# Pool issues its own loads, W1 goes first, W2 passes through y, and the last three chunks run as two halves of 256 rows

## The reference

```
h = sigmoid(einsum('bts,st->bs', x, W1) + b1)      # x: 1024 x 24 x 1024, W1: 1024 x 24
y = h @ W2.T + b2                                  # W2: 1024 x 1024, y: 1024 x 1024, all f32
```

## Time and profile before

| | us |
|---|---|
| median of 3 runs (lowest, highest) | 336.53 (336.32, 337.71) |
| the profiled execution's own time | 337.88 |
| its span, first to last instruction | 336.1 |
| PE busy | 273.2 (81%) |
| DVE busy | 259.1 (77%) |
| POOL busy | 165.5 (49%) |
| ACT busy | 44.5 (13%) |
| HBM read / written | 105.5 MB / 4.2 MB |

### The profile page before, as it was taken

How to read it: one execution, slowest core, us unless ns; L and a number is a source line. 1 busy time by engine, 2 the same in 40 slices (tenths; PEclk the granted TensorE clock), 3 DMA queues, 4 the chain that set the end, 5 groups by cost and what they waited for, 6 DMA issues and landing times.

```text
span 336.1 us, 4849 instructions
## 1 busy us (share of the span) xinstructions
PE 273.2 (81%) x1825; PEld 238.0 (71%) x1825; DVE 259.1 (77%) x386; ACT 44.5 (13%) x76; POOL 165.5 (49%) x63
## 2 busy tenths in 40 slices
PE   2672975696977989999993899998889979299896
PEld 2572965596966877889782788876778868188674
DVE  0652997987998979799993489899788997168836
ACT  1210220211260000012300000040101140000010
POOL 0050007679059684800899980049755059972000
PEclk9978797977999999999997699999999998789979
DMA  8999959999999999999957999999999992698006
GB/s 260 398 398 393 387 183 393 386 387 387 386 386 387 387 387 387 387 384 373 373 205 244 374 375 384 383 385 374 373 373 372 356 341 81 207 345 262 1 0 250
DMA packets 67383, 109.99 MB, mean 327 GB/s; under 512 B 3224, under 2 KB 40096, under 8 KB 67360
## 3 DMA queue, kind: packets, MB, share of 16 engines
q1 hardware_dynamic: 65584, 106.96, 89.3%
q10 hardware_dynamic: 1776, 2.72, 2.2%
HBM read 105.48 MB, written 4.19 MB: 326 GB/s over the span
## 4 chain that ended last, share of the span: by engine, by line
PE 36%; DMA 35%; POOL 14%; issue 10%; ACT 2%; SPq 1%; DVE 1%; POOLq 0%; DVEq 0%; ACTq 0%
DMA ring<-in_r_x 35%; PE xbank L207 17%; PE pbank L267 15%; POOL y L463 6%; POOL nsum L446 3%; PE xbank L301 3%; POOL h_lo L456 2%; POOL nsum L451 1%; POOL nat L448 1%; PE pbank L301 1%; ACT h L392 1%; SPq L171 1%; DVE acc L323 1%; ACT h_hi L421 0%; PE pbank L225 0%
## 5 line engine op out<-in xcount | busy, mean ns | idle before, releaser
L323 DVE SCALAR_TENSOR_TENSOR acc<-xbank,w,acc 128x512 f32<-128x512 f32 x304 | 213.6, 746 | 57.1 <-PE xbank L207 54.5
L207 PE MATMUL xbank<-ident,ring 128*128 128x128 f32 x1280 | 190.8, 286 | 54.5 <-DMA ring<-in_r_x 53.6
L207 PEld LDWEIGHTS xbank<-ident,ring 128*128 128x128 f32 x1280 | 162.2, 149 | 83.2 <-issue 33.0
L448 POOL TENSOR_TENSOR nat<-nat,w1all 128x2048 f32<-128x2048 f32 (+2 forms) x15 | 55.1, 3674 | 50.7 <-DMA nat<-in_r_x 50.7
L451 POOL TENSOR_TENSOR nsum<-nsum,nat 128x2048 f32<-128x2048 f32 (+2 forms) x15 | 55.4, 3692 | 1.2
L267 PE MATMUL pbank<-w_hi,h_hi 128*128 128x512 f32 x112 | 51.7, 462 | 0.0
L267 PE MATMUL pbank<-w_lo,h_hi 128*128 128x512 f32 x112 | 50.8, 454 | 0.0
L456 POOL TENSOR_TENSOR h_lo<-h,h_hi 128x512 fp32r<-128x512 f32 x14 | 17.5, 1283 | 67.5 <-ACT h_hi L421 67.5
L267 PE MATMUL pbank<-w_hi,h_lo 128*128 128x512 f32 x112 | 45.6, 454 | 0.0
L446 POOL TENSOR_TENSOR nsum<-nat,w1all 128x2048 f32<-128x2048 f32 (+2 forms) x5 | 18.5, 3699 | 18.7 <-DMA nat<-in_r_x 18.7
L392 ACT ACTIVATE h<-acc,b1col 128x512 f32<-128x512 f32 (+1 forms) x19 | 11.0, 646 | 104.1 <-DVE y L339 57.7
(11 more groups left out here) (38 smaller groups left out, 94.7 us busy)
## 6 DMA issues: line engine op xcount, KB each, us to landing
ring<-in_r_x SPq DMA_DIRECT2D x40, 1024.0 KB, 14.4
ring<-in_r_x SPq DMA_DIRECT2D x40, 768.0 KB, 11.6
ring<-in_r_x SPq DMA_DIRECT2D x20, 512.0 KB, 7.5
nat<-in_r_x SPq DMA_DIRECT2D x8, 1024.0 KB, 14.2
nat<-in_r_x SPq DMA_DIRECT2D x8, 768.0 KB, 10.0
y<-in_L_rec_W SPq DMA_DIRECT2D x1, 2048.0 KB, 18.3
out_y<-y ACTq DMA_DIRECT2D x4, 512.0 KB, 6.8
nat<-in_r_x SPq DMA_DIRECT2D x4, 512.0 KB, 6.6
```

The lines of the kernel that those rows point to most:

```text
L207: mm = pe.transpose(xbank[u % XBANKS][:, j * P:(j + 1) * P], tile[:, j, :], ident[:, :])
L323: nc.vector.scalar_tensor_tensor(out=acc[:, c, :], in0=xbank[u % XBANKS][:, :], scalar=w1[:, bass.ds((STAGES[i][1] + c) * T + t, 1)], in1= ...
L448: nc.gpsimd.tensor_tensor(slot, slot, row, ALU.mult).then_inc(nat_weighed, 1)
```

## The change

It does five things. POOL issues the loads of its own four t, each as soon as the slot has been used, so no `nat` load stands in SP's queue. W1 is the first transfer of SP's queue instead of ACT's first. Both halves of W2 pass through `y`, the second one once the first is turned: pieces 0 to 7 at units 14 to 35, pieces 8 to 15 at units 58 to 79. `b2` is added by POOL one stage sooner, behind the weighted sum and tile by tile. The second group is cut otherwise: 3 chunks, 2 chunks, and then the last 3 chunks for tiles 0 and 1 and again for tiles 2 and 3. There are now 84, 84, 63, 42, 63 and 63 units in stages 0 to 5, the last two with 2 transposes and 256 columns each. The span of the product steps goes from `units - 13` to four fifths of the units less the lead (10 units, 20 in the half stages).

```diff
 STAGES = (
-    (0, 0, 4, (3, 11, 15, 19)),
-    (0, 4, 4, (1, 6, 11, 16)),
-    (1, 0, 3, (1, 6, 11, 16)),
-    (1, 3, 3, (1, 6, 11, 16)),
-    (1, 6, 2, (1, 6, 11, 16)),
+    (0, 4, 0, 4, (2, 4, 10, 14), "keep"),
+    (0, 4, 4, 4, (0, 3, 10, 14), "last"),
+    (4, 4, 0, 3, (0, 3, 10, 14), "keep"),
+    (4, 4, 3, 2, (0, 3, 10, 14), "add"),
+    (4, 2, 5, 3, (0, 3, 10, 14), "last"),
+    (6, 2, 5, 3, (0, 3, 10, 14), "last"),
 )
...
         def steps_due(i, v):
-            lead, rest = 10, 3
-            span = len(units[i]) - lead - rest
-            return max(0, min(product_steps(i), -(-(v - lead + 1) * product_steps(i) // span)))
+            steps = outs[i - 1] * 3 * chunks[i - 1]
+            lead = 10 * JT // tiles[i]
+            span = (len(units[i]) * 4) // 5 - lead
+            return max(0, min(steps, -(-(v - lead + 1) * steps // span)))
...
+            def load(m):
+                i, t = divmod(m, NK)
+                j0, nj, c0, n, _, _ = STAGES[i]
+                pool.dma_start(nat[:, m % NATS, :nj, :n * P],
+                               x_v[:, j0:j0 + nj, t, c0 * P:(c0 + n) * P]).then_inc(nat_loaded[m % NATS], 16)
...
                         nc.gpsimd.tensor_tensor(ssum, slot, row, ALU.mult).then_inc(nat_freed, 1)
+                        if 1 <= m < NS * NK - 1:
+                            pool.wait_ge(nat_freed, m)
+                            load(m + 1)
                     else:
                         nc.gpsimd.tensor_tensor(slot, slot, row, ALU.mult).then_inc(nat_weighed, 1)
                         pool.wait_ge(nat_weighed, i * (NK - 1) + k)
                         pool.wait_ge(nat_freed, m)
+                        if 2 <= m + 1 < NS * NK:
+                            load(m + 1)
                         nc.gpsimd.tensor_tensor(ssum, ssum, slot, ALU.add).then_inc(nat_freed, 1)
...
+            pool.wait_ge(unit_turned, 1)
+            load(0)
+            load(1)
             for i in range(NS):
                 weighted_sum(i)
+                if i > 0 and fate[i - 1] == "keep":
+                    add_b2(i - 1)
                 if i < LAST:
                     low_parts(i)
-                if i in (1, 3):
-                    add_b2(i // 2)
```

More of the change, by code:

```diff
@@ L39, in rec_kernel @@
     XBANKS = 6
-    assert (B, T, S, O) == (2 * BANK, 24, 1024, 1024) and OUTS == 8
-    chunks = [s[2] for s in STAGES]
+    assert (B, T, S, O) == (2 * BANK, 24, 1024, 1024)
+    tiles = [s[1] for s in STAGES]
+    chunks = [s[3] for s in STAGES]
+    wide = [n * P for n in tiles]
+    fate = [s[5] for s in STAGES]
     units = []
-    ts = list(range(NK, T))
-    for g, c0, n, places in STAGES:
-        order = [("x", t, c) for t in ts[:-2] for c in range(n)]
+    for n in chunks:
+        order = [("x", t, c) for t in range(NK, T - 2) for c in range(n)]
         order += [("n", 0, c) for c in range(n)]
-        order += [("x", t, c) for t in ts[-2:] for c in range(n)]
+        order += [("x", t, c) for t in range(T - 2, T) for c in range(n)]
         units.append(order)
@@ L54, in rec_kernel @@
     first_h = [sum(chunks[:i]) for i in range(NS)]
+    outs = [OH * n for n in tiles]
+    first_out = [sum(outs[:i]) for i in range(NS)]
+    kept_at = [sum(n for n, f in zip(outs[:i], fate) if f == "keep") for i in range(NS)]
+    added_at = [sum(n for n, f in zip(outs[:i], fate) if f != "keep") for i in range(NS)]
     item_of, item_end = {}, []
     for i in range(NS):
-        for t in ts:
+        for t in range(NK, T):
             item_of[i, t] = len(item_end)
@@ L97, in rec_kernel @@
         nat_loaded = [sem(f"nat_loaded{n}") for n in range(NATS)]
-        w2_loaded = [sem(f"w2_loaded{n}") for n in range(3)]
+        w2_loaded = [sem(f"w2_loaded{n}") for n in range(OH)]
         w1_loaded = sem("w1_loaded")
@@ L126, in rec_kernel, with out_half @@
         block = ctx.enter_context(nc.Block())
-        def out_half(n):
+        def out_half(i, n):
             j, oh = divmod(n, OH)
[L130 to L142, removed]
+            return j, (STAGES[i][0] + j) % JT, slice(oh * BANK, (oh + 1) * BANK)
         def steps_due(i, v):
-            lead, rest = 10, 3
-            span = len(units[i]) - lead - rest
-            return max(0, min(product_steps(i), -(-(v - lead + 1) * product_steps(i) // span)))
+            steps = outs[i - 1] * 3 * chunks[i - 1]
+            lead = 10 * JT // tiles[i]
+            span = (len(units[i]) * 4) // 5 - lead
+            return max(0, min(steps, -(-(v - lead + 1) * steps // span)))
         def outs_due(i, v):
             return steps_due(i, v) // (3 * chunks[i - 1])
-        W2_FROM, W2_EVERY = 12, 3
         SETS = {4 + q: q for q in range(1 + NK)}
-        SETS.update({65 + 2 * q: 1 + NK + q for q in range(NK)})
+        SETS.update({38 + 2 * q: 1 + NK + q for q in range(NK)})
+        W2S = {14 + 3 * m if m < SC else 58 + 3 * (m - SC): m for m in range(OH * SC)}
         @block.sync
         def _(sp):
-            m = 0
-            for i, (g, c0, n, places) in enumerate(STAGES):
+            sp.dma_start(w1[:, :].rearrange("p (c t) -> p c t", t=T),
+                         W1.rearrange("(c p) t -> p c t", p=P)).then_inc(w1_loaded, 16)
+            for i, (j0, nj, c0, n, places, _) in enumerate(STAGES):
                 cols = slice(c0 * P, (c0 + n) * P)
@@ L164, in _ @@
                     before = sum(p < at for p in places)
[L165 to L173, removed]
+                    t = NK + at - before
+                    if at not in places:
                         q = item_of[i, t]
@@ L176, in _ @@
                             sp.wait_ge(unit_turned, item_end[q - RING] + 1)
-                        sp.dma_start(ring[:, q % RING, :, :n * P], x_v[g, :, :, t, cols]).then_inc(x_loaded[q % RING], 16)
+                        sp.dma_start(ring[:, q % RING, :nj, :n * P], x_v[:, j0:j0 + nj, t, cols]).then_inc(x_loaded[q % RING], 16)
                     if i == 0 and at == 1:
-                        sp.dma_start(h[:, :, :].rearrange("p (j a) b -> p j (a b)", j=2), w2_v[1][:, 0:2, :]).then_inc(w2_loaded[1], 16)
-                        sp.dma_start(nat[:, 1, :, :].rearrange("p (j a) b -> p j (a b)", j=2), w2_v[1][:, 2:4, :]).then_inc(w2_loaded[2], 16)
-                    if i == 0 and at == 4:
                         sp.dma_start(y[:, :, :], w2_v[0]).then_inc(w2_loaded[0], 16)
[L183 to L187, removed]
+                    if i == 0 and at == 17:
+                        sp.wait_ge(w2_turned, SC)
+                        sp.dma_start(y[:, :, :], w2_v[1]).then_inc(w2_loaded[1], 16)
+            for i in range(2, NS):
+                for n in range(outs[i] if fate[i] == "last" else 0):
+                    _, j, cols = out_half(i, n)
+                    sp.wait_ge(y_added, added_at[i] + n + 1)
+                    sp.dma_start(out_v[:, JT + j, cols], y[:, j, cols]).then_inc(stored, 16)
+            sp.wait_ge(stored, 16 * OH * JT)
             sp.wait_ge(group_stored, 16 * JT)
@@ L205, in turn_unit @@
                     tile = nsum[:, :, c * P:(c + 1) * P]
-                for j in range(JT):
+                for j in range(tiles[i]):
                     mm = pe.transpose(xbank[u % XBANKS][:, j * P:(j + 1) * P], tile[:, j, :], ident[:, :])
@@ L210, in turn_set @@
             def turn_set(q):
-                if q >= 2:
+                half, k = divmod(q - 1, NK)
+                if q == 1 + NK:
+                    pe.wait_ge(w_lo_ready, SC)
+                elif q >= 2:
                     pe.wait_ge(set_kept, q - 1)
@@ L245, in product_step @@
                 n, r = divmod(k, 3 * nch)
[L246 removed]
+                j, _, cols = out_half(b, n)
                 if r == 0:
@@ L310, in add_unit @@
                 kind, t, c = units[i][v]
-                n = chunks[i]
+                n, rows = chunks[i], slice(0, wide[i])
+                weight = w1[:, bass.ds((STAGES[i][2] + c) * T + t, 1)]
                 dve.wait_ge(unit_turned, u + 1)
```

179 lines of the change are left out of this document (81 added, 98 removed).

## The result

The changed kernel takes **353.25 us** (median of 4 executions; 352.39 to 354.86), the kernel before 337.12 in the same session: a ratio of 1.0485, 95% interval 1.0436 to 1.0534. So it is **slower by 4.9%**, where 331.5 us and a gain were forecast, and it lies beyond the range of 322 to 344. It went the way of the first rival, POOL's loads, but for another reason than that rival gave.

What follows compares the result with a forecast made beforehand. Transfers bound stage 1, PE's product phase and POOL's b2 block the second group. Last unit at 317.2 us plus a 13.8 tail gives a span of 331.0; plus 1.8, less 1.35, 331.5 us, range 322 to 344.

Steps and rivals of the forecast that it cites:

- the first rival: POOL's loads cost too much: gain gone at 1.7 us per issue, 349 us at 2.6; chance 0.16.
- POOL's chain of loads: Stages 1 to 5: three links of issue, landing, multiply; PE waits 2.9 us in stage 4, 0.7 in stage 5.
- the landing L: Time for POOL's load to land: 6.5, 5, 3.6, 3.2, 3.2 us in stages 1 to 5, up to 9.7 to 6.3.
- The issue s: POOL's time to issue one load: 1.2 us for 512 rows, 1.0 for 256.
- PE comes to "n": When PE reaches the units needing POOL's sum: 57.0, 48.6, 35.1, 27.1, 24.3 us into stages 1 to 5.
- Part 1: Stage 0: SP's 13.5 us wait goes, but the item behind W2 lands at 68.6; stage 1 begins 93.0, against 93.9.
- Part 2: Stages 1 and 2: 65.2 and 54.8 us, against 65.7 and 61.5; stage 2 ends 8.1 us ahead.
- Part 3: Stages 3 to 5: 104.2 us instead of 98.4; half units each 0.39 us, 1.5 us per half stage for PE's clock.
- Part 4: The tail: 48 matmuls become 36, so 16.6 us becomes 13.8.
- Slower transfers for all: Rival: loads issued by POOL slow all transfers; at 10% stage 0 is 6.6 us longer, 340 us; chance 0.04.
- Half units that do not overlap: Rival: at 0.48 us per half unit stages 4 and 5 are 9 us longer, 339 us; chance 0.06.
- The chain hides and PE keeps its clock: Rival: 3.6 us of lateness and 3 of clock go, and stage 0 gives 2: 323 us; chance 0.20.

Runs made afterwards that it cites:

- experiment 9: Changed kernel with three ring slots instead of six, so SP has at most three loads in flight beside POOL's: 373.27 us in a single execution.
- experiment 1: Changed kernel, but POOL issues load m+2 at the end of step m, not load m+1 between multiply and add: 323.78 us, 0.9624 of the kernel before.
- experiment 7: As experiment 1, with POOL's loads 4 and 5 held in stage 0 until PE has turned 60 units: 322.42 us, 0.9582 of the kernel before.
- Experiment 2: Kernel before, with only b2 added sooner, before the low parts and tile by tile: 320.31 us, ratio 0.9521.
- experiment 6: Changed kernel with POOL's loads a step ahead and the second group in whole tiles (3, 3, 2 chunks): 319.83 us, 0.9513 of the kernel before.

## Why the prediction was wrong

**The step that failed is "POOL's chain of loads", and in it the landing L above all.** The prediction wrote the chain down, with its place and what is queued behind it, and priced PE's waits at 3.6 us, in stages 4 and 5 only. They came to 34.2 us, in all of stages 1 to 5. Its own sign of being wrong, waits of more than 2 us in stages 1 to 3, was met three times. Three things were off.

- *L was taken from the wrong end.* The prediction had two rows for 512 KB, 3.6 us with nothing ahead and 7.0 beside SP's full queue, and stayed near 3.6 because "transfers have time to spare". They had, on average; but SP refills its slots as they come free, so a load of POOL's nearly always has some of SP's beside it, and with fewer of those in flight (experiment 9) the landings were shorter. Issue and landing together, three such links a stage, took 27.5, 25.5, 20.5, 17.1 and 16.6 us, where 23.1, 18.6, 14.4, 12.6 and 12.6 stood. That is 25.9 us. L by itself was 8.4, 7.7, 6.1, 5.0 and 4.8 on average where 6.5, 5, 3.6, 3.2 and 3.2 were taken: longer in every stage, and in every stage below the upper end that the prediction gave.
- *The issue s was taken too high*: 0.79 us for 512 rows and 0.74 for 256, not 1.2 and 1.0. So the rival named the right wait and the wrong price: it asked for s over 1.7, and the time was lost with s at 0.8. The s that the prediction worked out and left out, 0.4 above SP's 0.37, comes close. Before every issue but the first of a stage there is also 0.30 us from the multiply's end, which I had not counted.
- *PE comes to "n" sooner.* It stood ready 53.2, 45.1, 32.2, 25.3 and 22.1 us after the starts of stages 1 to 5, not 57.0, 48.6, 35.1, 27.1 and 24.3. These are 14.1 us, more than the whole slack of stages 1 to 3. Of them 5.9 are DVE's: it had done what stands before "n" that much sooner than I had summed. The other 8.2 are PE's lead, which I had left out: it may run up to six banks ahead of DVE, and was 1.2 to 2.1 us ahead in each stage.

The sums were whole 59.0, 50.9, 39.1, 33.1 and 29.4 us after the stages' starts, 25.6 us later in all than forecast. (The links and the gaps of 0.30 us are 30.1; POOL's first multiplies, 3.2 us sooner in all, and the cheaper fourth issue, 1.5, stand against it, and some tenths are left.) PE's turn began 0.14 us after each sum, 0.7 in all. Together: 25.6 + 0.7 later, 14.1 sooner, less 9.7 of slack, plus the 3.6 foreseen, give 34.3, where 34.2 was measured. The span was 20.1 us over the forecast (351.1 against 331.0): some 30.6 of waits that were not foreseen and 1.0 in stage 0, less about 11 that the other parts were shorter.

Some sums of the prediction are slightly off, and none of them decides: by its own terms the sum of stage 2 is whole at 43.6, not 43.9; the two half stages add to 30.4 and 27.6, not 30.6 and 27.8; and the smaller s would have taken 1.6 us from the time, not some 3.

**Part 1 held.** Stage 0 ended at 94.0 (93.0 forecast), and W2's second half is where the 13.5 us went: PE waits for the ring item behind it until 68.43, where 68.6 was forecast. Experiments 1 and 7 show that what POOL loads ahead of it costs 6 us there.

**Part 2 held in its gain.** Less the waits stages 1 and 2 take 62.8 and 53.0, against 65.2 and 54.8. Experiment 2 gives the sooner `b2` 17 us in the kernel before. Of these I saw 6.7 in stage 2; the 10 of stage 4 I had seen as well (37.9 for 48.6), but the new cut of the group took that stage's place.

**Part 3 held in its pace and not in its clock.** Half units ran at (9.88 - 0.475)/24 = 0.39 us, the value taken, each 0.475 long:

```profile
305.95 9.88 DVE L309 SCALAR_TENSOR_TENSOR acc<-xbank,w,acc 128x256 f32<-128x256 f32 x25
```

Less the waits stages 3 to 5 take 38.5, 29.7 and 26.7, where 39.2, 32.1 and 29.3 stood. I had added 1.5 us to each half stage for a clock of 0.90. The means of the two stages are 0.91 and 0.90, but that is luck. From 267.0 to 292.3 and from 304.7 to 326.9, the stretches before the waits, the granted clock is 1.00, the higher of its two levels, with PE busy for 24.91 of 25.30 and 21.91 of 22.20 us. It is 0.79 and 0.78 in the waits, and 0.61 in the 4.4 and 4.5 us after them. In experiment 1, without the waits, the two stages have 0.94 and 1.00. So the clock fell with the waits, and the half stages did not bring it down by themselves to what was assumed. What they do cost is 4 us against whole tiles (experiment 6).

**Part 4** was 1.5 us too careful (12.3 against 13.8).

**The rivals.** Slower transfers for all did not come: slices 1 to 16 keep their rate. The rule about engines 7 and 15 that the rival takes from the Trainium skill ("DMA: Bandwidth & Descriptors", "Latency and other measured facts"), and that this page calls a best guess, would have made stages 0 and 1 longer. Stage 0 ends where it did (94.0 against 93.9), and stage 1 is longer only by its wait, so no run here shows such a loss. Half units that do not overlap are out. "The chain hides and PE keeps its clock" is what experiment 1 is, at 323.8 where 323 was given for it. That the numbers meet is luck: its stage 0 ends at 99.65 and not at 91, and the later stages make up for it.

## What to carry to other kernels

When an engine loads for itself into two slots, write down its program as a chain and ask at which point the slot is really free: the next load for that slot belongs there, so that a whole step of work hides its landing, and not between two halves of a step that wait for it. Take the landing from a row measured beside the traffic that will be there, not from an idle queue. Compare the chain's end with the position of the engine that waits for it, which can be ahead of its consumer by the buffers between them. A long operation in front of a blocking queue is worth moving first: that alone gave 5%.

## What the runs showed of the hardware

POOL's issue of a load cost it 0.74 us for 384 KB (256 rows) and 0.79 us for 512 KB to 1 MB (512 rows) (medians by stage of the changed kernel). POOL's loads do not queue up behind all that SP has issued: 1 MB landed in 9.0 to 9.2 us in stage 1 of the changed kernel, where SP's own `nat` loads of that size, in SP's queue, took 14.2 (median) by the profile's page of the kernel before.
